# Keeping the turned x for both users, splitting weights earlier, and a shorter ring of row tiles, in a kernel of two attention layers and two mixtures of experts

## The reference, cut to what matters

```python
x = x + _layernorm(_L0_attn_ref(_layernorm(x), wq, bq, wk, bk, wv, bv, wo, bo))   # linear attention
x = x + _layernorm(_L0_ffn_ref(_layernorm(x), sg_w, su_w, sd_w, router_w, routing_bias, wg, wu, wd))
x = x + _layernorm(_L1_attn_ref(_layernorm(x), Wq, bq, Wk, bk, Wv, bv, Wo, bo))   # softmax attention
x = x + _layernorm(_L1_ffn_ref(_layernorm(x), gate_w, W1, W2, Ws1, Ws2))

# a mixture (L0; hidden width 512, L1: routed 192 and shared 384, softmax weights, no bias)
shared = silu(xt @ sg_w.T) * (xt @ su_w.T) @ sd_w.T
logits = xt @ router_w.T + routing_bias
topk_p, topk_idx = top_k(sigmoid(logits), 2)          # 2 of 8 experts for each row
h = silu(xt @ wg[e].T) * (xt @ wu[e].T)               # for each chosen expert e
out = shared + sum_e w[e] * (h @ wd[e].T)
```

## Time and profile before

| | us |
|---|---|
| time, median of 3 runs (2046.53 to 2051.81) | 2046.61 |
| the profiled execution's own time | 2046.28 |
| its span | 2044.1 |
| opening | 33.05 |
| `projected_residual` of layer 0, then `split_scaled` | 67.10, then 12.78 |
| `router_logits`, then `route`, layer 0 | 29.51, then 22.92 |
| `shared_expert`, then `routed_experts`, layer 0 | 142.87, then 333.82 |
| `projected_residual` of layer 1, then `split_scaled` | 86.51, then 10.23 |
| `router_logits`, then `route`, layer 1 | 29.64, then 20.99 |
| `shared_expert`, then `routed_experts`, layer 1 | 129.13, then 161.00 |

### The profile page before, as it was taken

How to read it: one execution, slowest core, us unless ns; L and a number is a source line. 1 busy time by engine, 2 the same in 40 slices (tenths; PEclk the granted TensorE clock), 3 DMA queues, 4 the chain that set the end, 5 groups by cost and what they waited for, 6 DMA issues and landing times. The chain is left out here.

```text
span 2044.1 us, 43859 instructions
## 1 busy us (share of the span) xinstructions
PE 1667.6 (82%) x15250; PEld 953.9 (47%) x15250; DVE 1477.2 (72%) x2895; ACT 1098.1 (54%) x2248; POOL 418.3 (20%) x533
## 2 busy tenths in 40 slices
PE   2897259999999993767999999999997358889950
PEld 1775148976666662321222222222225247767740
DVE  4776677764444446869999999999936776656657
ACT  1443415643333332534999999999993415444422
POOL 2000206631222222220000000000000206534432
PEclk9998759999999996776999999999998759999985
DMA  5600004541111113332121111120005003323445
GB/s 200 276 0 6 31 1 153 157 125 48 60 58 61 58 53 127 119 94 54 37 60 48 47 47 45 48 60 24 17 17 175 24 1 110 113 87 120 126 148 174
DMA packets 113033, 164.09 MB, mean 80 GB/s; under 512 B 20246, under 2 KB 89756, under 8 KB 110556
## 3 DMA queue, kind: packets, MB, share of 16 engines
q1 hardware_dynamic: 97340, 117.85, 19.1%
q0 software_dynamic: 15520, 43.93, 5.9%
HBM read 89.07 MB, written 72.37 MB: 79 GB/s over the span
## 5 line engine op out<-in xcount | busy, mean ns | idle before, releaser
L1499 DVE TENSOR_REDUCE sa_row_max<-psum 128x1 f32<-128x1024 f32 x512 | 582.5, 1217 | 12.3 <-PE psum L1381 12.2
L1482 ACT ACTIVATE sa_probs<-psum 128x512 f32<-128x512 f32 x1024 | 549.6, 597 | 37.8 <-PE psum L1432 28.3
L1381 PE MATMUL psum<-v_k_max,v_q_stack 48*128 48x512 f16 x1024 | 301.4, 398 | 24.4 <-DVE sa_row_max L1499 16.2
L1412 PE MATMUL psum<-sa_probs,sa_v_now 128*32 128x256 f32 (+1 forms) x3840 | 321.0, 406 | 0.1
L1432 PE MATMUL psum<-v_q_stack,sa_k_main 49*128 49x512 f16 x1024 | 309.8, 384 | 2.0 <-ACT sa_probs L1482 1.2
L1993 PE MATMUL psum<-m0w_all,m0fx_xt_high 128*128 x568 | 193.4, 382 | 0.6 <-DVE m0fx_xt_low L1925 0.6
L1432 PEld LDWEIGHTS psum<-v_q_stack,sa_k_main 49*128 49x128 f16 x1024 | 64.6, 94 | 222.3 <-ACT sa_probs L1482 208.5
L1412 PEld LDWEIGHTS psum<-sa_probs,sa_v_now 128*32 128x32 f32 x3840 | 75.7, 108 | 189.9 <-issue 100.1
L1939 DVE TENSOR_TENSOR m0fx_ht_low<-psum,m0fx_ht_high 128x512 f16<-128x512 f32 x71 | 49.1, 692 | 134.4 <-ACT m0fx_ht_high L1907 134.4
L1901 ACT ACTIVATE m0fx_gate<-psum 128x512 f32<-128x512 f32 x71 | 42.4, 598 | 152.7 <-PE psum L1993 148.4
L1884 POOL DMA_INDIRECT y_rows<-m0fx_y_sb,m0fx_x_in x71 | 68.3, 962 | 274.1 <-DVE m0fx_y_sb L1946 274.1
(11 more groups left out here) (371 smaller groups left out, 3737.6 us busy)
## 6 DMA issues: line engine op xcount, KB each, us to landing
x_rows<-la_blank SPq DMA_DIRECT2D x18, 1032.0 KB, 8.2
v_q_stack<-q_scratch SPq DMA_DIRECT2D x192, 64.0 KB, 2.4
m0fx_x_in<-x_rows SPq DMA_DIRECT2D x71, 129.0 KB, 2.0
m1fx_x_in<-x_rows SPq DMA_DIRECT2D x71, 129.0 KB
m0fs_stage<-in_up SPq DMA_DIRECT2D x16, 512.0 KB
m0g_got<-y_rows SPq DMA_DIRECT2D x32, 256.0 KB, 3.8
o_scratch<-sa_o_sb POOLq DMA_DIRECT2D x32, 256.0 KB, 2.5
wo_o_in<-o_scratch SPq DMA_DIRECT2D x32, 256.0 KB, 3.6
```

Source lines behind the costliest of these rows:

```text
L1381: nc.tensor.matmul(mx_ps[m % 2][:, half * 512:(half + 1) * 512], q_stack[h][side:side + ROWS, head, qt * P:(qt + 1) * P], k_max[side:side ...
L1412: last = nc.tensor.matmul(o_ps[32 * g:32 * g + 32, cols], v_now[:, kt, kv, :], probs[(GROUPS * step + g) % 16][:, cols], start=(kt == 0), ...
L1482: nc.scalar.activation(probs[at % 16][:, :], st_ps[bank_of(at)][:, :], ACT.Exp, scale=0.25 / (QK_SCALE * QK_SCALE)).then_inc(s["expd"], 1)
L1499: nc.vector.tensor_reduce(row_max[n % 2][:, at % QT, column:column + 1], mx_ps[m % 2][:, :], AX.X, ALU.max).then_inc(s["maxed"], 1)
```

## The change

- The opening's two stages become one. SP issues x batch 0, the two weight DMAs, then batches 1 to 3. Statistics, aggregation and the power go batch by batch (8 columns each), and the weights' high and low parts are made between them.
- `projected_residual` raises x's 32 columns to the power in two pieces, 0 to 23 (started in step 15) and 24 to 31.
- The stages `split_scaled` are gone. The weights of the shared expert and the router are loaded by DMAs that SP issues at the end of its list in `linear_attention` and in `softmax_attention` (`SharedGiven`), and split in four parts inside `projected_residual`: in layer 0 one part a step (ACT in steps 0 to 3, DVE in steps 1 to 4), in layer 1 ahead of the first step (`SharedWeights`).
- `router_logits` writes the turned pair of all 32 tiles into the memory of y (`core.xt`), and takes the logits with the bias, the maxima and their indices in rounds of four groups. `route` starts at `index_f`. The bias is loaded in `router_logits`.
- `shared_expert` reads `core.xt`; its turning, high and low are gone. Its loop is written out whole.
- `routed_experts` holds 6 row tiles, not 8, and `hidden` is written over `gate`; `silu` waits for the turning of the hidden layer two tiles back.

The core of the diff:

```diff
+        self.xt = self.y[:, :, :].bitcast(F16).rearrange("p t (a k q) -> p t a k q", a=2, k=KD)
...
+                for b in range(1, B):
                     sp.dma_start(core.x[:, b * TB:(b + 1) * TB, :], x_dram[b, :, :, :]).then_inc(x_in[b], 16)
+
+            @block.scalar
+            def _(act):
+                for k in range(KD):
+                    act.wait_ge(w_in[k], 16)
+                    nc.scalar.activation(w_high[:, k, :], given[:, k, :], ACT.Copy).then_inc(high_done, 1)
 
             @block.vector
             def _(dve):
                 for b in range(B):
+                    at = slice(b * TB, (b + 1) * TB)
...
                         nc.vector.bn_stats(stats.halves[:, i, :], core.x[:, i, :]).then_inc(x_stats, 1)
-                dve.wait_ge(x_stats, T)
-                stats.aggregate(dve, 0, T, 0, core.mean_var[:, :, 0], 0.5)
...
+                    stats.aggregate(dve, b * TB, TB, b, core.mean_var[:, at, 0], 0.5)
+                    if b < KD:
+                        dve.wait_ge(high_done, b + 1)
+                        nc.vector.tensor_tensor(w_low[:, b, :], given[:, b, :], w_high[:, b, :].bitcast(F32),
...
+                for b in range(B):
+                    at = slice(b * TB, (b + 1) * TB)
+                    stats.rstd(pool, core.rstd[:, at], b * TB, TB, b, core.minus_half[:, at], eps_added, rstd_done)
+                pool.wait_ge(rstd_done, B)
...
+    X_PIECES = (slice(0, 24), slice(24, T))
...
-                pool.wait_ge(rstd_done, len(GROUPS_OF) + 1)
+                for n, at in enumerate(X_PIECES):
+                    pool.wait_ge(var_done, len(GROUPS_OF) + (n + 1))
+                    nc.gpsimd.tensor_tensor(core.rstd[:, at], var[:, at], core.minus_half[:, at], ALU.pow)\
+                        .then_inc(rstd_done, 1)
...
+                    for n in range(shared.PARTS):
+                        shared.scalar_high(act, n)
...
+                    if o_dram is None and step < shared.PARTS:
+                        shared.scalar_high(act, step)
...
+                def norm_x(n):
+                    at = X_PIECES[n]
+                    dve.wait_ge(x_counted, at.stop)
+                    dve.wait_ge(rstd_done, next(m for m, (a, b) in enumerate(GROUPS_OF) if at.stop <= 2 * b) + 1)
+                    variance(x_halves, core.mean_var[:, :, 0], at, 0.5)
...
+                    if o_dram is None and 0 <= step - 1 < shared.PARTS:
+                        shared.vector_low(dve, step - 1)
...
-                dve.wait_ge(x_counted, T)
-                dve.wait_ge(rstd_done, len(GROUPS_OF))
-                variance(x_halves, core.mean_var[:, :, 0], slice(0, T), 0.5)
+                    if step == PAIRS - 1:
+                        norm_x(0)
...
+                coming.sync_load(sp)
...
+    def sync_load(self, sp):
+        for n, source in enumerate(self.sources):
+            sp.dma_start(self.part(n).rearrange("p (k f) -> p k f", k=source.shape[1]), source)\
+                .then_inc(self.loaded, 16)
+
...
+    def scalar_high(self, act, n):
+        act.wait_ge(self.given.loaded, 16 * self.PARTS)
+        self.nc.scalar.activation(self.part(0, n), self.given.part(n), ACT.Copy, scale=W_SCALE)\
+            .then_inc(self.high_done, 1)
+
+    def vector_low(self, dve, n):
+        dve.wait_ge(self.high_done, n + 1)
+        self.nc.vector.scalar_tensor_tensor(out=self.part(1, n), in0=self.given.part(n), scalar=W_SCALE,
+                                            in1=self.part(0, n), op0=ALU.mult, op1=ALU.subtract)\
+            .then_inc(self.low_done, 1)
+
...
-    PEELED = 1
...
-        xt = [[ph.sb(f"xt_{x}{j}", [P, KD, P], F16) for x in ("high", "low")] for j in range(2)]
...
-            for k in range(PEELED):
-                turn(k)
-            with eng.Fori(PEELED, TURNS - PEELED) as k:
-                turn(k)
-            for k in range(TURNS - PEELED, TURNS):
+            for k in range(TURNS):
                 turn(k)
...
-                def turn(i, j, w):
-                    pe.wait_ge(s["x_ready"], i + 1)
-                    ge(pe, s["xt_low"], i - 1)
-                    for k in range(KD):
-                        last = nc.tensor.transpose(xt_ps[j][:, k * P:(k + 1) * P], x_in[w % UNROLL][:, 0, k * P:(k + 1) * P],
-                                                   core.ident[:, :])
-                    last.then_inc(s["x_turned"], 1)
-
...
-                def up(out, j, column):
+                def up(out, i, column):
...
-                        pe.wait_ge(s["xt_low"], i + 1)
                         ge(pe, s["silu_done"], i - 1)
-                        up(gate_ps[j], j, F).then_inc(s["gated"], 1)
+                        up(gate_ps[j], i, F).then_inc(s["gated"], 1)
                         ge(pe, s["hidden_done"], i - 1)
-                        up(lin_ps[j], j, 0).then_inc(s["lined"], 1)
-                    if real(i + 2):
-                        turn(i + 2, j, u + 2)
+                        up(lin_ps[j], i, 0).then_inc(s["lined"], 1)
                     if real(i - 1):
                         down(i - 1, 1 - j)
-                turn(0, 0, 0)
-                turn(1, 1, 1)
...
-    ROWS_HELD = 8
+    ROWS_HELD = 6
...
-                    ge(act, s["hidden_done"], i - 1)
+                    ge(act, s["h_turned"], i - 1)
...
-                    nc.vector.scalar_tensor_tensor(out=hidden[j][:, :], in0=lin_ps[j][:, 0:F], scalar=H_SCALE / W_SCALE,
+                    nc.vector.scalar_tensor_tensor(out=gate[j][:, :], in0=lin_ps[j][:, 0:F], scalar=H_SCALE / W_SCALE,
                                                    in1=gate[j][:, :], op0=ALU.mult, op1=ALU.mult)\
                         .then_inc(s["hidden_done"], 1)
...
-                if bias_row is not None:
-                    dve.wait_ge(bias_in, 16)
-                    then(nc.vector.tensor_tensor(r.logits[:, :, :], r.logits[:, :, :],
-                                                 bias[:, :].unsqueeze(1).to_broadcast([P, T, E]), ALU.add))
-                for t in range(T):
-                    last = nc.vector.max(top[:, t, :], r.logits[:, t, :])
-                then(last)
-                for t in range(T):
-                    last = nc.vector.max_index(index[:, t, :], top[:, t, :], r.logits[:, t, :])
-                then(last)
...
+                    if g % ROUND == 0:
+                        ge(pe, s["kept"], g // ROUND - 1)
...
+                def maxima(q):
+                    dve.wait_ge(s["kept"], q + 1)
+                    for t in tiles_of(q):
+                        last = nc.vector.max(top[:, t, :], logits[:, t, :])
+                    last.then_inc(s["maxed"], 1)
...
+                def find(q):
+                    dve.wait_ge(s["maxed"], q + 1)
+                    for t in tiles_of(q):
+                        last = nc.vector.max_index(index[:, t, :], top[:, t, :], logits[:, t, :])
+                    last.then_inc(s["found"], 1)
...
-                    route(core, name + "r", r, normalise, bias_row)
-                shared_expert(core, name + "fs", w_shared, x_rows, r, w, (up_r, down_r), filled)
+            with Phase(nc, name + "l") as pl:
+                top = pl.sb("top", [P, T, 8])
+                index = pl.sb("index", [P, T, 8], mybir.dt.uint32)
+                router_logits(core, name + "rl", shared.router, bias_row, top, index)
+                route(core, name + "r", r, normalise, top, index)
+            shared_expert(core, name + "fs", shared.w, x_rows, r, w, (up_r, down_r), filled)
             routed_experts(core, name + "fx", w, x_rows, y_rows, r.expert_of)
-        yield r
```

320 lines of the change are left out of this document (140 added, 180 removed).

## The result

The changed kernel takes 2091.45 us (median of 4, 2086.22 to 2097.44), the kernel before 2049.17 in the same comparison: a ratio of 1.021, with a 95% interval from 1.018 to 1.024. It is slower by 42 us where the forecast was 24. The profiled execution took 2097.44, so its trace is read against the 2046.28 of the trace before. These two executions are 51 us apart, the medians 42: differences read between the traces add up to 9 us more than the change of the medians.

A forecast was written before the change was run, and what follows sets the result against it. Limits differ by stage: loads and barriers in some, PE in `routed_experts`, where the ring's loop decides. All other terms sum to -53.9, layer 1's ring adds +78, giving +24: 2070 us, range 2044 to 2106 for 8 in 10.

The forecast's parts named there:

- its own case: Whole kernel: the ring of 6 binds at full clock; 2052 to 2088 us, chance 0.62.
- rivals 1 and 3: Ring binds with clock falling, at most 2121, chance 0.18; ring binds and instruction gaps eat savings, 2092 to 2134, 0.08.
- The ring, layer 1: `routed_experts`, layer 1: with 6 row tiles PE waits in a loop of 6.46 to 6.76 us for two tiles; +78.
- The ring, layer 0: `routed_experts`, layer 0: 6 row tiles suffice, 0.85 us to spare, with a few late loads; +2 (0 to 8).
- Savings: All stages expected to get shorter, opening through `shared_expert` of layer 1: 55.9 us less in all.
- `shared_expert`, layer 0: Dropped transposes save 0.22 x 32 = -7.0, the chain ahead of the first matmul -1.6; -8.6 in all.
- `shared_expert`, layer 1: Dropped transposes save -7.0, and -3 of PE's gaps and waits for hidden low parts; -10 (-7 to -16).
- `linear_attention`: 0: The `linear_attention` stage of layer 0: no change in time forecast.
- Opening, power in two pieces, the splits, the router: Opening -5.3; projection with splits -13.7 (layer 0) and -12.6 (layer 1); `router_logits` and `route` -3.7 and -2.0.
- The ring binds and the clock falls: `routed_experts`, layer 1: PE's clock falls to half, loss up to +129 instead of +78, 2121 at most; chance 0.18.
- The ring doesn't bind: `routed_experts`, layer 1: store and load take under 1.9 us together, so no loss; 1992, chance 0.12.
- rival 3: `shared_expert` written out, both layers: PE runs out of instructions, gaps add 22 to 64 us; 2092 to 2134, chance 0.08.

The follow-up runs named there:

- e2_rows7: The changed kernel with 7 row tiles instead of 6, each load waiting for the store seven tiles back: 2019.1 us, ratio 0.986 to the kernel before.
- e3_before_rows6: The kernel before with 6 row tiles and nothing else altered: 2145.36 us, ratio 1.047 to the kernel before.
- e1_rows8: The changed kernel with 8 row tiles in both routed stages and nothing else altered: 1998.53 us, ratio 0.975 to the kernel before.
- e6_order: The changed kernel with 8 row tiles and the next weights' splits moved behind the hidden parts in `shared_expert`: 1985.58 us, ratio 0.968 to the kernel before.
- e9_both: e6_order, 8 row tiles, plus the ring of tails (small buffers for each row's address and weight) from e4: 1994.4 us, ratio 0.973 to the kernel before.
- e10_onepiece: e6_order with x's power behind both projections as one piece of 32 columns: 1999.84 us, ratio 0.976 to the kernel before.
- e5_loop: The changed kernel with 8 row tiles and the six middle turns of `shared_expert` in a loop again: 1998.61 us.
- e7_turn: The changed kernel with 8 row tiles, but `shared_expert` as before the change, turning x on PE in a loop: 2008.5 us, ratio 0.980 to the kernel before.
- e8_open: The kernel before with the new opening alone: 2039.34 us, ratio 0.996 to the kernel before.
- e4: The changed kernel, 6 row tiles, POOL copying each row's address and weight into small buffers, so loads wait for no store: 1996.82 us, ratio 0.975 to before.

## Why the prediction was wrong, point by point

The direction was right, and the mechanism: the earlier trace rows held it all. The time lay inside the range, but not inside the range that the forecast had for its own case, 2052 to 2088; above that, the range had been widened for rivals 1 and 3, and neither happened. That 2091 falls inside is luck. What failed is the size of the change, 42 where 24 was forecast, since the forecast is a small difference of two large terms (+80 and -56 give +24), and both were off to the same side.

- **The ring, layer 1: the term "6.46 to 6.76 for two tiles".** This is the step that failed. The loop was measured as 7.07: 2.51 from store to load, 2.39 from load to turning, 2.17 from turning to store, over tiles 6 to 70. I built it from single values and a median: 2.42, 2.04 and 2.0 to 2.30. The third link was right; the first two came out 0.44 longer together. The median of load to turning is 2.15, near what I took, but the mean is 2.39. PE stood waiting for the load at 51 of the 65 turnings, with a mean of 2.26 and at most 3.80. At the other 14 PE did not wait for it (mean 2.86, at most 4.21); many of them stand right behind a late tile, as 42, 53 and 58 do, for the loops of the odd and the even tiles share PE. A chain in which each link waits for the last pays the mean of each. It made +91.8 out of +78. The trace before could have given it: its store to load has a mean of 2.82 in layer 1 (2.56 in layer 0), where I took the first value, 2.42, and its loads in layer 0 that have a landing take 2.1 on average and 3.43 at most. With those means the loop comes to an estimated 7.0 to 7.3. e2_rows7 and e3_before_rows6 bear out the sum of means as the rule (7.53 for three tiles, 7.12 for two).
- **The ring, layer 0: "it holds, with a few late loads: +2 (0 to 8)".** It was +8.1 in this trace, +5.3 in e3_before_rows6. The slack of 0.85 was right: the schedule leaves 2.90 from load to turning. But +2 stood without a working. The delays add up to 8.0: some 3.9 behind five stores that took 3.5 to 4.8 to release their load, some 3.3 behind six loads that took 3.3 to 3.7 to the turning, and the rest behind the tiles after them.
- **Savings: -56 forecast, -49.6 by e1_rows8.** In the trace the stages with a forecast give -52.2; `linear_attention`'s +5.0 and -1.0 elsewhere make it -48.2.
- **`shared_expert`, layer 0: "0.22 x 32 = -7.0, and -1.6".** Only -5.2. A turning gone saves 0.22 if PE is the bound afterwards; in one slot of four it now waits some 0.3 for DVE's hidden low part, which stood behind the split of the next weights. On PE, after the 48 up matmuls, the wait in the changed kernel:

```profile
379.86 0.28 PE L1798 MATMUL psum<-m0s_all,m0fs_ht_high 128*128 128x256 f16 x1
```

The matmul before it started 0.37 earlier, where the next follows within 0.06 otherwise. So 16.86 us for four slots became 16.29, not 15.98. e6_order took that wait away and has 15.96, which is the forecast's value. But e9_both and e10_onepiece, in the same order and also without that wait, have 15.96 to 16.4, and e5_loop in the old order has 16.06: the wait is one cause, and not the only one. How much the order is worth in the total, 4 to 13 us, the runs leave open.
- **`shared_expert`, layer 1: "-3 of them".** The 3 did not come. The stage gave 7.2, and that this is near the turnings' 7.0 is luck as far as the traces tell: between two kernels that both loop, e7_turn and e5_loop, the turnings are worth 1.5 of it. The gaps came to 8.3 us in 24 after the change. The Trainium skill ("Runtime: NRT & Kernel Launch", Instruction fetch mechanics) tells of a fetch stall at a taken branch whose target lies outside the two pages held. In the total no such cost can be seen (e5_loop and e1_rows8 are 0.1 us apart); in layer 1's stage e5_loop is 2.8 longer, in layer 0's 4.5 shorter, and what does either is not shown.
- **`linear_attention`: 0, measured +5.0.** PEclk was 0.94 there and not 0.97, and PE was busy 120.3 us for the 608 matmuls that took 115.1 before: three stretches at half clock (under e8_open). e8_open and e10_onepiece show the stage at 141.7 and 141.6 behind the same opening, so the change need not bring this with it; what decides it is open.
- **Opening, power in two pieces, the splits, the router.** -6.8, -13.8, -11.5, -4.7 and -3.0 against -5.3, -13.7, -12.6, -3.7 and -2.0. The splits in the first steps of the projection were covered about as the earlier trace rows said.
- **Rivals.** "The ring binds and the clock falls" was at most a small part: PEclk was 0.92 over the stage, and from 1900 to 1950 it was 1.00, while the stores of tiles 33 to 46 started in the 45.0 us from 1901.07 to 1946.08, 3.46 a tile, against 3.52 over the whole loop; that leaves an estimated 4 us of the 92 for the clock. Its price had a slip: 71 x (4.14 - 2.28) is 132, not 129. "The ring doesn't bind" is excluded by e1 and e4. The gaps of rival 3 did not grow with the change (8.8 us before, 8.3 after). The Trainium skill ("DMA: Bandwidth & Descriptors", Anatomy of one DMA) gives, for a DMA issued from GpSimd, about 2.0 us fixed and adds the bytes divided by 436 GB/s. The prediction left out the second part, an estimated 0.3 us for 129 KB. The loads here, which SP issues, took 2.00 at the least and 2.39 in the mean from issue to turning.

The version to keep, as far as the runs tell, is the changed kernel with 8 row tiles and with the weights' splits behind the hidden parts, with the ring of tails or without: 1985.6 (e6_order) and 1994.4 (e9_both), 63 and 54 below the kernel before.

## What to carry to other kernels

Before a ring of buffers is shortened, write down the whole loop that frees one (use, result, store landed, next load landed, use) and divide it by the tiles it spans; a ring can be free of cost only while that quotient, taken with the mean latencies and not the medians or the least, is under the work of a tile. Where it is under by little, single slow transfers still cost: layer 0 with 6 rows had about 4.3 against 4.55 and lost 5 to 8 us. If the loop is too long, ask which reader holds the buffer last: here it was eight bytes a row read by the store, and copying them out opened the loop with no larger ring of row tiles. And when a forecast is the difference of two large terms, its range must carry the errors of both.
